# Third stage of a fused transformer block: side products spread over the 32 steps by another rule

## What is computed

```python
def _L1_attn_ref(x, norm_scale, split_scale, Wq, Wk, Wv, Wo):   # 8 heads of 64, 2 key/value groups
    nrm = jnp.linalg.norm(x, axis=-1, keepdims=True) * d ** (-0.5)
    h = norm_scale * x / (nrm + EPS) * split_scale
    q, k, v = h @ Wq.T, h @ Wk.T, h @ Wv.T                      # then split into heads and groups
    scores = jnp.einsum('bghsd,bgtd->bghst', q, k) / np.float32(np.sqrt(dh))
    out = jnp.einsum('bghst,bgtd->bghsd', jax.nn.softmax(scores, axis=-1), v)
    return x + out @ Wo.T                                       # after merging the heads
```

## Time and profile before

| | |
|---|---|
| median of 3 runs | 1582.69 us (1582.68 to 1584.97) |
| the profiled execution | 1585.42 us, span of its instructions 1583.6 us |
| mean granted clock of PE | 0.975 |
| busy share of the span | PE 92%, PEld 75%, DVE 64%, ACT 52%, POOL 46% |
| instructions | 21336 |
| chain that ended last | PE 59%, DVE 9%, POOL 4%, ACT 2% |
| third stage, first score to last score | 338.43 to 963.71 us |

### The profile page before, as it was taken

How to read it: one execution, slowest core, us unless ns; L and a number is a source line. 1 busy time by engine, 2 the same in 40 slices (tenths; PEclk the granted TensorE clock), 3 DMA queues, 4 the chain that set the end, 5 groups by cost and what they waited for, 6 DMA issues and landing times.

```text
span 1583.6 us, 21336 instructions
## 1 busy us (share of the span) xinstructions
PE 1454.8 (92%) x7252; PEld 1189.2 (75%) x7252; DVE 1019.0 (64%) x2050; ACT 818.1 (52%) x1562; POOL 725.6 (46%) x963
## 2 busy tenths in 40 slices
PE   5999999588999999999999987599899999999996
PEld 4888778467787878787877876477687888888884
DVE  6888788658888888888888776354423423424233
ACT  4666556358778787868686864322222213212221
POOL 4788546534445454545454445132333333243332
PEclk9999999889999999999999999699999999999998
DMA  7555022410002020202020201222010010110100
GB/s 203 134 155 134 21 94 80 153 60 1 1 1 80 1 80 1 80 1 80 1 81 1 100 1 54 93 82 85 1 54 27 27 53 0 53 53 0 53 27 27
DMA packets 46205, 88.51 MB, mean 56 GB/s; under 512 B 2720, under 2 KB 3744, under 8 KB 46112
## 3 DMA queue, kind: packets, MB, share of 16 engines
q1 hardware_dynamic: 42416, 79.98, 14.7%
q0 software_dynamic: 3696, 7.34, 2.8%
HBM read 62.14 MB, written 25.17 MB: 55 GB/s over the span
## 4 chain that ended last, share of the span: by engine, by line
PE 59%; DVE 9%; POOL 4%; issue 3%; ACT 2%; DMA 2%; SPq 0%; POOLq 0%; DVEq 0%; ACTq 0%
PE f_inner L57 23%; PE g_side L1533 12%; PE f_down L1944 9%; PE g_score L57 5%; PE g_turned L1553 5%; PE g_output L1581 2%; PE g_output L1579 2%; DVE g_ptl L1457 2%; DVE g_neg_max L1443 2%; DVE f_wl L1868 1%; POOL g_prob L1168 1%; DMA x_pair<-x_mixed 1%; PE f_inner L1916 1%; POOL g_power L1142 1%; DVE g_q L1372 1%
## 5 line engine op out<-in xcount | busy, mean ns | idle before, releaser
L1168 POOL TENSOR_SCALAR g_prob<-g_prob,g_inv_sum 128x512 f32<-128x512 f32 x256 | 177.8, 694 | 310.8 <-DVE g_inv_sum L1448 310.7
L57 PE MATMUL f_inner<-f_xth,f_wh 128*128 128x512 f32 x704 | 281.1, 399 | 15.6 <-DVE f_wl L1868 12.7
L57 PE MATMUL f_inner<-f_xtl,f_wh 128*128 128x512 f32 x704 | 279.7, 397 | 0.0
L1778 ACT ACTIVATE f_silu<-f_inner,f_inner_scale 128x512 f32<-128x512 f32 x88 | 60.6, 689 | 414.3 <-PE f_inner L57 414.3
L1837 DVE SCALAR_TENSOR_TENSOR f_hidden<-f_inner,f_inner_scale,f_silu 128x512 f32<-128x512 f32 x88 | 66.0, 750 | 314.0 <-PE f_inner L57 314.0
L1726 POOL TENSOR_TENSOR f_hl<-f_hidden,f_hh 128x512 fp32r<-128x512 f32 x88 | 127.9, 1453 | 297.3 <-DVE f_hh L1843 297.3
L1443 DVE TENSOR_REDUCE g_neg_max<-g_score 128x1 f32<-128x512 f32 x256 | 175.2, 685 | 86.5 <-PE g_score L57 85.3
L1277 ACT ACTIVATE g_prob<-g_score,g_neg_max 128x512 f32<-128x512 f32 x256 | 176.7, 690 | 99.5 <-DVE g_neg_max L1443 97.4
L1457 DVE TENSOR_TENSOR g_ptl<-g_turned,g_pth 128x512 fp32r<-128x512 f32 x256 | 173.6, 678 | 14.5 <-ACT g_pth L1319 12.5
L1553 PE MATMUL g_turned<-identity,g_prob 128*128 128x128 f32 x1024 | 155.8, 275 | 25.8 <-DVE g_ptl L1457 25.8
L57 PEld LDWEIGHTS f_inner<-f_xth,f_wh 128*128 128x128 f32 x704 | 133.3, 189 | 54.5 <-DVE f_wl L1868 17.3
(11 more groups left out here) (232 smaller groups left out, 3393.3 us busy)
## 6 DMA issues: line engine op xcount, KB each, us to landing
xt<-x_t SPq DMA_DIRECT2D x16, 512.0 KB, 5.9
x_mixed<-x_resident SPq DMA_DIRECT2D x8, 1024.0 KB, 4.3
x_pair<-x_mixed SPq DMA_DIRECT2D x8, 1024.0 KB, 7.7
g_res<-x_mixed SPq DMA_DIRECT2D x8, 1024.0 KB, 6.5
x_attended<-g_res SPq DMA_DIRECT2D x8, 1024.0 KB, 5.1
x_pair<-x_attended SPq DMA_DIRECT2D x8, 1024.0 KB, 5.6
x_resident<-x SPq DMA_DIRECT2D x7, 1024.0 KB, 11.4
factor_sum<-factors POOLq DMA_DIRECT2D x7, 1024.0 KB, 10.5
```

The costliest lines, as they stand in the source:

```text
L57: last = nc.tensor.matmul(out, lhsT, rhs, start=(n == 0), stop=(n == len(pairs) - 1))
L1168: nc.gpsimd.tensor_scalar(prob[:, at, :], prob[:, at, :], inv_sum[:, at:at + 1], 1.0, ALU.mult, ALU.mult).then_inc(prob_ready, 1)
```

## The change

Three constants and the rule of `side_schedule` change:

```diff
-H = (5, 6, 10, 11)
-CONVERT = (20, 24, 32, 39)
-SHARE, SHARE_BESIDE_OUT = 8, 4
+H = (5, 6, 9, 11)
+CONVERT = (22, 24, 32, 39)
+SHARE, SHARE_LATER, SHARE_BESIDE_OUT = 5, 8, 4
...
-    at = 0
+    at = room = 0
     for u in range(UNITS):
         shares.append([])
-        room = SHARE_BESIDE_OUT if (u - OUT_LAG) % T < 2 else SHARE
-        while waiting and room > 0:
+        room = min(room, 0) + (SHARE_BESIDE_OUT if (u - OUT_LAG) % T < 2 else SHARE if u < 2 * T else SHARE_LATER)
+        while waiting and room >= 0.5:
...
             earliest += {"wo0": [CONVERT[-1] - UNITS + 2], "k": [end.get("h3", 0) + 3],
-                         "h0": [H[0] + 2], "h1": [H[1] + 2]}.get(name, [])
+                         "h0": [H[0] + 3], "h1": [H[1] + 3], "h2": [H[2] + 3], "h3": [H[3] + 3]}.get(name, [])
...
-            step = min(count - at, max(1, int(room / cost)))
+            step = min(count - at, max(1, int(room / cost + 0.5)))
```

## The result

| | before | after |
|---|---|---|
| median of 4 runs | 1583.83 us (1582.68 to 1585.22) | 1601.93 us (1601.39 to 1606.19) |
| ratio to before | | 1.0123, 95% interval 1.0107 to 1.0139 |
| profiled execution, its span | 1585.42, 1583.6 us | 1602.29, 1600.4 us |
| third stage, first to last score | 625.3 us | 639.9 us |

What follows compares the result with a forecast made beforehand. PE was taken to bound a batch, so only waits could change. Waits of 6.2 + 2.4 - 0.3 - 2.3 = +6.0 us and clock falls of +3.1 on 1582.7 gave 1591.8 us, range 1583 to 1601.

Steps and rivals of the forecast that it cites:

- segment A: Score of step 28 to score of the next step 2: longer by 0.89 us (+0.5 to +1.3), seven times.
- falls of the clock there: At changes of batch: the longer wait drops PE's clock at two of seven, 1.57 us each, +3.1 (0 to 11.0).
- segment B: Score of step 2 to step 9: stays 17.0 us, set by the chain from statistics over POOL's scales to ACT.
- segment C: Score of step 9 to step 21: longer by 0.4 us (-0.6 to +1.0) in six batches, +2.4.
- D, S21 to S28: Score of step 21 to score of step 28: same shares for PE and no wait, zero change.
- batch 0 to its step 28: First batch: q3's lower part later (+1.4), five passes fewer in steps 0 to 6 (-1.2): -0.3 us (-2 to +1.5).
- batch 7 from its step 2: Last batch: new shares in steps 7 and 15 save most of a clock fall or bare step: -2.3 us (-4 to 0).
- The step that failed: Whole kernel: instruction counts and SP's transfer order stay, so PE's work stays and only waits can come or go.
- the wait of the score of step 0 for q0's lower part: Change of batch: score of step 0 starts 3.04 us after that of step 31, a wait of 2.1 instead of 1.5.
- the waits of segment C: Steps 9 to 21: waits at step 10, h1, step 11, wo0 and h3 (1.1 us), sum 2.4 us for 1.5.
- The clock term: Changes of batch: PE's clock falls at two of seven, +3.1 us in the sum (bounds 0 and 11.0).

Runs made afterwards that it cites:

- e1: The changed kernel with the load of x issued on SP ahead of the store that waits for the last addition: 1594.41 us, ratio 1.0054.
- e2: The kernel before with the load of x issued on SP ahead of the store: 1584.65 us, ratio 0.9994.
- e3: The kernel before with its normalisation and addition of the output one step later, PE's plan untouched: 1598.73 us, ratio 1.0084.
- e10: The kernel before's shares in steps 0 to 14, the changed kernel's in 16 to 26, q0 ended at 28, early load of x: 1589.40 us, ratio 1.0031.
- e4: The kernel before with q0's last four passes moved from step 28 to 29 and four more from 27 to 28: 1597.43 us, ratio 1.0084.
- e5: The changed kernel with the early load of x and q0 ended in step 28 as before: 1589.87 us, ratio 1.0029.
- e12: The kernel before with the early load of x, in the order k, q0, v with v from step 26: 1580.07 us, ratio 0.9980.
- e6: The changed kernel with the early load of x and the order k, q0, v in place of k, v, q0: 1589.23 us, ratio 1.0025.
- e9: The kernel before with NORM and ADD one step later and the load of x ahead of the store: 1588.40 us, ratio 1.0025.

## Why the prediction was wrong

By the segments and the profiled executions (+16.8 us of span), term by term:

| term | predicted | measured |
|---|---|---|
| segment A, seven times | +0.89 each, 6.2 | +0.86 each, 6.0 |
| falls of the clock there | two, 3.1 | two, 3.2 |
| segment B, batches 1 to 6 | 0 (-1.3 to +0.4 each) | +6.3, in batches 2, 4, 6 |
| segment C, six times | +0.4 each, 2.4 | +0.62 each, 3.7 |
| D, S21 to S28 | 0 | 0 |
| batch 0 to its step 28 | -0.3 | -2.3 |
| batch 7 from its step 2 | -2.3 | -2.2 |
| before the first and behind the last score | 0 | +2.2 |

The first row's 6.0 and the third's 6.3 are the two large ones, and I had only the first. In batch 0, 1.6 of the 2.3 lie between its first two scores (3.30 and 1.73), and e1, with the plan of the kernel after, has 3.10 there, so most of that is not the plan's. In batch 7 the number came out partly by luck: e2, with the shares of the kernel before, takes 66.79 from its step 2 to the last score where the kernel before took 67.96, as no clock falls there in e2.

**The step that failed** is the sentence that nothing but PE's waits can change because "SP's transfers keep their order, and the store that follows ADD one step later has ten steps before the next use". It looked at what the store's data are used for and not at what stands behind the store in the queue. SP works through its program in order: the load of x for the batch after next stands behind that store, and its reader is DVE in step 0. The rows for it were in the trace before: issue at 565.06, landing 7.7 us later, statistics at 572.98, 0.2 us behind it; and the list of waits had 0.8 us in three places. That is a load with nothing to spare. One step of 2.7 us later, less the 1.5 us by which the change delays step 0 itself, is 1.2 us late, which is what four of the five waits show (0.99 to 1.41); the fifth is 3.4, by the load that took 10.1. e1 and e3 show it from both sides. Segment B was the place: its chain begins with those statistics, and the prediction wrote "statistics of the next tile in step 2" without asking what they wait for.

What held: the wait of the score of step 0 for q0's lower part, 3.04 predicted and 2.98 measured; that PE's own work does not set segment B (17.0 in each batch that the load does not disturb, with three passes more in it); the waits of segment C in kind (h1's step 2.82, wo0's 3.08, and 3.42 from score 17 to score 18, where h3 waits for `total_of` of wo1; e10 shows that without that bank the light steps 15 and 16 would still wait, for DVE); nothing between steps 21 and 28. Segment C was sized low: the wait of wo0 measured 0.35 for 0.2, h1's two together 0.6 for 0.5, and the segment cost 0.2 more a batch. The clock term was right in its number by chance as much as by reason: e4 has five falls with the same wait, the kernel after two, e5 none with 1.5. The Trainium skill's advice (TensorE: Matmul & The Clock Gate, "Why this matters for your kernels") warns only of longer gaps. Read as leave to ignore shorter ones, it does not hold here: an idle time of 1.84 behind the transposes of a bare step was followed by half rate. That q0 and v could trade places without giving the time back elsewhere was not foreseen; e12 shows it for the kernel before, all but 0.4 of 1.5 us a batch, and e6 that it does not hold for the changed one, where half comes back.

Left open: why the medians of after and e1 differ by more (about 11 us by the ratios) than their segments B (6.2) in the one profiled execution each. The runs' own clocks go some way: the four of the kernel after had a mean granted clock of 0.970 to 0.972, those of e1 0.972 to 0.976, and the profiled one of e1 was its slowest. The means differ by 0.0028 of 1600 us, which I estimate at 4 us; where the clock fell in the other executions is not recorded. Open too are the 2.2 us outside the third stage's scores. Between kernels with the same first two stages the first score starts anywhere from 338.4 to 342.1 us, so 0.5 of them need not be the change's; the 1.7 behind the last score go with a granted clock there of 0.96 in place of 0.97.

## What to carry to other kernels

When a step moves, go through each queue from the moved instruction down: what waits behind it on the same queue counts, not only what reads its result. A transfer that lands just in time shows next to no wait (here 0.8 us in all) and has no slack; before moving its issue, compare issue and landing with its reader. And a price for a wait of TensorE is not complete without the clock: a wait of 2 us cost 0.6 us more than before in one batch and 2.2 in the next.

## What was not expected of the hardware

One wait of 1.84 us before a score, behind a bare step, left the clock at 1.00 in some batches and was followed by 0.53 to 0.70 in others: two of seven in the kernel after and in e1, five of seven in e4. Why there and not elsewhere is not shown. A wait of 1.28 in the same place never did it, in 7 changes of the kernel before, and one of 1.70 not in the 12 changes of e3 and e9 that have it. And a fall may be free of further cost: in batches 3 and 5 of the kernel after, the slowed PE hid the late load.
